# ViT block on one core: second-layer chunks, weight pieces and late attention steps moved within the first FFN's order

## The reference, cut to what matters

```python
h = einsum('bhid,oi,od->bho', x, weighted_sum, weight)      # x (8, 512, 256, 4) -> h (8, 512, 256)
h = h + attn(layernorm(h))                                  # 16 heads of 16, rope, unit q and k, softmax, projection
# FFN with 8 experts, hidden size 1024, every expert on every token, weighted by its gate
x_flat = layernorm(h)
probs = sigmoid(x_flat @ Wg + bg); weights = probs * (probs > 0.5)
hid = relu(einsum('td,edh->eth', x_flat, W1) + b1)
out = einsum('te,etd->td', weights, einsum('eth,ehd->etd', hid, W2) + b2)
h = h + out
```

## Time and profile before

| what | value |
|---|---|
| three runs | 1892.27, 1889.27 and 1893.55 us; median 1892.27 us |
| the profiled execution | 1891.92 us, of which the span from first to last instruction 1890.1 us |
| TensorE matmuls (PE) | 96% of the span busy |
| VectorE (DVE) | 69% |
| ScalarE (ACT) | 57% |
| GpSimd (POOL) | 6% |
| mean granted TensorE clock | 0.989 |

### The profile page before, as it was taken

How to read it: one execution, slowest core, us unless ns; L and a number is a source line. 1 busy time by engine, 2 the same in 40 slices (tenths; PEclk the granted TensorE clock), 3 DMA queues, 4 the chain that set the end, 5 groups by cost and what they waited for, 6 DMA issues and landing times.

```text
span 1890.1 us, 33337 instructions
## 1 busy us (share of the span) xinstructions
PE 1813.9 (96%) x13036; PEld 1173.0 (62%) x13036; DVE 1312.3 (69%) x2469; ACT 1076.7 (57%) x1658; POOL 111.6 (6%) x92
## 2 busy tenths in 40 slices
PE   5689899999999999999999999999999999999999
PEld 4157445775567655776557755677556775566666
DVE  7868645688865888558875788758886588863333
ACT  3745777446654566446664466544765456654444
POOL 1013323200000000000000000000000000000000
PEclk9789999999999999999999999999999999999999
DMA  4332552415122331234312242221512323223221
GB/s 166 112 112 90 147 180 99 168 51 151 69 89 101 84 140 68 69 121 113 112 68 90 79 134 90 89 98 71 156 68 70 121 70 111 89 72 117 92 104 42
DMA packets 103979, 192.40 MB, mean 102 GB/s; under 512 B 67448, under 2 KB 80656, under 8 KB 87440
## 3 DMA queue, kind: packets, MB, share of 16 engines
q1 hardware_dynamic: 103824, 190.28, 30.5%
HBM read 153.55 MB, written 20.97 MB: 92 GB/s over the span
## 4 chain that ended last, share of the span: by engine, by line
PE 81%; DVE 5%; issue 3%; ACT 3%; DMA 2%; DVEq 0%; ACTq 0%; SPq 0%
PE bank_h L1069 32%; PE bank_f L1088 11%; PE bank_f L1090 10%; PE bank_f L1091 10%; PE bank_o L975 4%; PE bank_s L950 4%; PE bank_s L855 3%; PE bank_s L856 3%; PE bank_s L857 3%; DMA qt<-probs 2%; ACT hh L832 1%; PE bank_m L987 1%; PE bank_s L1023 1%; PE bank_m L864 1%; PE bank_o L864 1%
## 5 line engine op out<-in xcount | busy, mean ns | idle before, releaser
L1069 PE MATMUL bank_h<-x,w1s 128*128 128x512 f16 x3072 | 749.7, 381 | 2.4 <-ACT hh L832 2.4
L829 ACT ACTIVATE h<-bank_h,b1s 128x512 f32<-128x512 f32 x512 | 352.2, 688 | 539.9 <-PE bank_h L1069 470.3
L1088 PE MATMUL bank_f<-w2s,hh 128*128 128x256 f16 x2048 | 560.2, 274 | 6.0 <-DVE acc L1362 5.9
L1090 PE MATMUL bank_f<-w2s,hh 128*128 128x256 f16 x2048 | 558.4, 273 | 0.0
L1091 PE MATMUL bank_f<-w2s,hl 128*128 128x256 f16 x2048 | 558.3, 273 | 0.0
L1069 PEld LDWEIGHTS bank_h<-x,w1s 128*128 128x128 f16 x3072 | 289.3, 99 | 296.2 <-issue 23.2
L1144 DVE TENSOR_TENSOR hl<-h,hh 128x512 f16<-128x512 f32 x448 | 309.9, 695 | 136.6 <-PE bank_f L1091 107.0
L832 ACT ACTIVATE hh<-bank_h,b1s 128x512 f16<-128x512 f32 x512 | 349.7, 683 | 0.0
L1088 PEld LDWEIGHTS bank_f<-w2s,hh 128*128 128x128 f16 x2048 | 201.3, 98 | 106.9 <-issue 48.0
L1090 PEld LDWEIGHTS bank_f<-w2s,hh 128*128 128x128 f16 x2048 | 200.6, 98 | 49.7 <-issue 0.3
L1091 PEld LDWEIGHTS bank_f<-w2s,hl 128*128 128x128 f16 x2048 | 200.4, 98 | 23.3
(11 more groups left out here) (215 smaller groups left out, 1800.2 us busy)
## 6 DMA issues: line engine op xcount, KB each, us to landing
w1s<-w_parts SPq DMA_DIRECT2D x56, 1024.0 KB, 4.8
w2s<-w_parts SPq DMA_DIRECT2D x56, 1024.0 KB, 4.8
raw<-in_w_dram SPq DMA_DIRECT2D x16, 1024.0 KB, 6.3
xraw<-in_x_t_dram SPq DMA_DIRECT2D x30, 512.0 KB, 6.1
w_parts<-w1s SPq DMA_DIRECT2D x8, 1024.0 KB, 8.8
w_parts<-w2s SPq DMA_DIRECT2D x8, 1024.0 KB, 10.6
out_dram<-acc SPq DMA_DIRECT2D x16, 256.0 KB, 6.0
w1s<-in_x_t_dram SPq DMA_DIRECT2D x2, 512.0 KB, 9.0
```

What stands on the lines that cost most here:

```text
L829: act.activation(h32[n % 2][:], bank_h[n % 2][:, :], ACT.Relu, bias=b1s[:, e, m:m + 1]).then_inc(h_hi.sem, 1)
L1069: last = pe.matmul(bank_h[n % 2][:, :], w[:, wp, k, m * P:(m + 1) * P], x16s[fb % 2][:, xp, k, :], start=(k == 0 and wp + xp == 0), stop=( ...
L1088: pe.matmul(o, high, w[:, 0, m, :], start=(m == 0 and t % 2 == 0), stop=False, skip_group_check=True)
L1090: pe.matmul(o, high, w[:, 1, m, :], start=False, stop=False, skip_group_check=True)
```

## The change

It changes only the list of the first FFN (the second of the four lists), and how ScalarE reorders it:

- `behind=(2 * HM, 3 * HM)`: `f2 16` stands behind `f1 20`, directly ahead of `f2 17`, and `f2 24` stands behind `f1 28`, directly ahead of `f2 25`.
- `exps_first` takes `maxima`, `share` and `scales` out of ScalarE's list, on which it does nothing, so that more steps are neighbours, and a `parts` step now also lets a following `f1` (its two relus) pass. On ScalarE this puts `f1 9` ahead of `parts 9`, `f1 12` ahead of `parts 11`, `f1 21` ahead of `parts 12`, `f1 22` ahead of `parts 14`, `f1 23` ahead of `parts 15`, `f1 30`, `f1 38` and `f1 46` ahead of `parts 18`, `22` and `26`, and the exps of `scores` 1, 3, 13, 25 and 27 ahead of the relus of `f1` 26, 27, 34, 42 and 43. The lists of batches 1 to 7, and the one that stands ahead of the first FFN, come out as before.
- `att_turn 3` stands ahead of `split_ahead 0` and `f2 50`, and with it `project 3` ahead of `parts 31` and `f2 51`.
- For expert 7, `share 7` and `scales 7` stand ahead of `f1 51` and `project 0`.

```diff
-FIRST_ATT = [0.0, 1.7, 2.5, 3.4]
+FIRST_ATT = [0.0, 1.7, 2.5, 2.85]
...
-              6: (0.6, 2.0, 3.2, 3.5, 4.3, 5.0, 5.7, 6.4)}.get(e, (0.6, 2.0, 3.7, 3.9, 4.4, 5.0, 5.7, 6.4))
+              6: (0.6, 2.0, 3.2, 3.5, 4.3, 5.0, 5.7, 6.4),
+              7: (0.6, 2.0, 2.95, 2.97, 4.4, 5.0, 5.7, 6.4)}.get(e, (0.6, 2.0, 3.7, 3.9, 4.4, 5.0, 5.7, 6.4))
...
-    def merge(waiting, done=0):
+    def merge(waiting, done=0, behind=()):
...
-            if c >= LAG:
+            if c >= LAG and c - LAG not in behind:
+                if c - LAG - 1 in behind:
+                    order.append(("f2", c - LAG - 1))
                 order.append(("f2", c - LAG))
...
-    return first, merge(attention_order(first_ffn=True) + prep, done=4), merge(attention), merge([])
+    return first, merge(attention_order(first_ffn=True) + prep, done=4, behind=(2 * HM, 3 * HM)), merge(attention), merge([])
...
-    order = list(order)
-    for passed, step in (("parts", ("scores",)), ("f1", ("scores", "gates"))):
+    order = [step for step in order if step[0] not in ("maxima", "share", "scales")]
+    for passed, step in (("parts", ("scores", "f1")), ("f1", ("scores", "gates"))):
```

## The result

The changed kernel runs in a median of 1896.3 us (1892.92 to 1897.93, 17 runs), the kernel before in 1892.46 us (1889.27 to 1894.39, 17 runs beside it). The ratio is 1.0016, with a 95% interval of 1.0009 to 1.0023: 3.0 us slower, 1.7 to 4.4 (the two medians themselves lie 3.8 us apart). That lies within the 0.2% of "no change", on the slow side of it, and 4.3 us above the upper end of the range that was given. The profiled execution took 1895.68 us, 0.6 under the median.

What follows compares the result with a forecast made beforehand. TensorE, busy 96% of the span, bounds the kernel, so only its waits can be won. Gains of 0.7 (front) and 2.5 us (attention turn) take 3.2 off 1891.92, 1888.7; median put at 1889.0 us, range 1885.7 to 1892.0.

Steps and rivals of the forecast that it cites:

- What bounds, and which waits go: First FFN: TensorE busy 96%; listed waits of 8.1 us plus 1.7 us of lower clock, 9.8 us at most to win.
- that rival: Raw loads landing late before share 4 and share 7: up to 4.8 us cost, 1893.9 us; chance 0.07.
- I take 1.9: VectorE's chain up to scales 3: 1.9 us late because pieces 9 and 11 stand behind relus; bounds 0 and 2.8.
- 2.6 us less the lateness: Front part, up to share 4 and f2 24: gain is 2.6 us less the lateness of VectorE's chain, 0.7 us left.
- The rule: VectorE and GpSimd instructions exclude each other on SBUF; moved chain meets subtractions at better places, lateness 1.2 us, sum 1888.3.
- A new wait of 0.7: Before mix_ahead 1: TensorE there at 338.85, split's first low half ends at 339.6; 2.4 to 2.5 us gain left.
- The prediction's own sign of being wrong: Wrong if scales 3 ends near 202.2, or the first FFN's end moves by less than 2 or over 4.5 us.
- 1.7 us more: At project 3: with its wait cut from 1.82 to 0.65, the clock stays at 2.4 GHz, gaining 1.7 us.
- the clock falls elsewhere: Clock falls before f1 24 or still at project 3: 1.7 us lost, partly covered, 1890.5 us; chance 0.15.
- the chain does not matter: VectorE makes up its lateness; the front gives up to 2.6 us, together 5.1: 1887.2 us; chance 0.30.
- The minor steps: share 7 sooner: a wait of 0.5 to 0.6 replaces 0.64, 0.2 us gained; f2 16 moved: 1.3 us taken alone.
- the step gives 1.3 us: f2 16 behind f1 20: f1 20 fills the wait for acc 1, worth 1.3 us taken alone.

Runs made afterwards that it cites:

- late_pass: Changed kernel, but relus pass pieces only from piece 12 on, so pieces 9 and 11 stand where they stood before; 1.0009 of the kernel before.
- low_on_dve: Changed kernel with the low halves of hidden chunks 54 to 56 made on VectorE instead of GpSimd; 0.9985 of the kernel before.
- att_only: Kernel before with only att_turn 3 and project 3 sooner; 1.0020 of the kernel before.
- share_only: Kernel before with only share 7 and scales 7 sooner; 0.9993 of the kernel before.
- behind_only: Kernel before with only f2 16 moved behind f1 20 and f2 24 behind f1 28; 0.9987 of the kernel before.
- split_first: Changed kernel with split_ahead 1 ahead of ln2 on VectorE; 0.9996 of the kernel before.

## Why the prediction was wrong

- **What bounds, and which waits go: right.** Every wait of the earlier trace rows went or shrank but the one before `f1 24`, whose growth was forecast too, and new ones stand at the steps named. `share 3` waits 1.58 us (1.4 predicted), `share 4` 1.29 (1.3), `share 7` 0.53 (0.5 to 0.6), `project 3` 0.75 (0.65) at the full clock. The raw loads landed in time: `maxima 9` began 220.09 - 213.27 = 6.8 us after low piece 15 was made, as before; that rival can be dropped.
- **"I take 1.9" for the lateness of VectorE's chain: mis-sized.** It is 3.1, or 2.8 without the later start of this execution, the upper bound that the prediction had given. The part worked out from relus and pieces was right: `late_pass`, which puts just that back, returned 1.95 us of it. What failed is the sentence that put `scales 3` behind the chain by that sum alone. Chunk 21's relus pass piece 12, its subtraction on GpSimd comes earlier with them and holds the stack's lows for 1.0 us. So `f1 24` started at 209.10 instead of 207.85, after a wait of 2.91 instead of 2, and the front's "2.6 us less the lateness" became a loss of 0.15 us at `f1 29` instead of a gain of 0.7.
- **The rule was weighed with the wrong sign.** The rows at `gw` showed the hold, and I guessed that a moved chain would meet the subtractions at *better* places (1.2 us of lateness). It met them at worse ones, at 202 us and again at 330, 334 and 339 us. The rule itself held: the low pieces went from 1.28 us to 2.18 and 2.24 beside a GpSimd subtraction, and back to 1.28 when the subtraction was taken off GpSimd. The Trainium skill (SBUF — State Buffer, "Who interferes with whom") says that a VectorE instruction with two SBUF inputs contends with a GpSimd instruction that reads SBUF. The trace agrees. Where the subtractions fall has to be worked out, and they had moved with the relus.
- **"A new wait of 0.7" before `mix_ahead 1`: the step that failed most.** It measured 2.44. I had carried `ln2` and `split_ahead 1` over with "the same pieces and adds ahead of it as before". They are the same, but pieces 30 and 31 took 1.9 us more together and the normed rows 0.9, while the one hold of before, 0.95 in `y`, was gone: 1.8 us more in all, and the wait was forecast 1.7 too short. TensorE was there at 339.2, near the 338.85 reckoned. `mix_ahead 1` went from 341.94 to 341.63, 0.6 us sooner when counted from the first mix, the missing fall included, where 2.4 to 2.5 were to be left. `low_on_dve` shows this cause, and `att_only` that the step on its own loses 3.8 us. The prediction's own sign of being wrong came out, the end of the first FFN moving by less than 2 us.
- **"1.7 us more" for the clock at `project 3`: a chance taken for a property.** The kernel before has that fall in its profile; `share_only`, with the same wait of 1.83 us, has none. The change then brought a wait of 2.44 us at `mix_ahead 1`, and with it more time at the lower clock (0.9872 against 0.9883 without that wait). The rival "the clock falls elsewhere" had the mechanism, priced at one fall in place of another, not at more falls than before.
- **The rival "the chain does not matter"** falls: VectorE made nothing up.
- **The minor steps: one held, one in part.** `share 7` sooner is worth 0.4 us in the trace of `share_only`, where 0.2 was forecast (by the time 1.3, -0.4 to 2.8). Of the two moved `f2`, "the step gives 1.3 us" for `f2 16` holds only as a shift: in `behind_only` these 1.3 us stand before `f1 23`. Its gain by the time is 2.5 us (0.8 to 4.2), where its expectation had 1.4.

## What to carry to other kernels

When steps are moved on one engine, list what its results start on the *other* engines, and look which instructions those will now run beside: a 1.2 us subtraction on GpSimd was worth 0.9 to 1.0 us of VectorE's chain at each of four places, and one edit that kept three of these off VectorE's way returned 5.9 us. Which of the two engines pays turned here on who began first, by 0.1 or 0.2 us. A wait can cost more than its length, because the clock may fall at it; but that isn't told by the length alone, for 3.1 us before `f1 23` cost no clock that the means of the runs show, and 2.44 at `mix_ahead 1` did. And a fall seen in one profile is one throw: compare runs at the same granted clock before giving it a price.

If a version is to be kept, it is the changed kernel with `split_ahead 1` ahead of `ln2` and with relus passing no pieces before piece 12, or none at all: 0.9980 and 0.9982 of the kernel before, about 0.9965 of the changed one. Not tried: filling the wait of 2.8 to 3.1 us before `f1 23` or `f1 24`, which is the largest that is left in them.

## What was not expected of the hardware

- A low piece on VectorE and a subtraction on GpSimd that began together, or GpSimd 0.12 us ahead, cost VectorE 0.90 to 0.96 us and GpSimd next to nothing: its own took 1.21 and 1.16 us, where the mean of the 64 is 1.19. With VectorE 0.22 us ahead (the kernel before at 329.73) it was the other way round: 1.28 us for VectorE, 2.07 for GpSimd.
- The same wait is followed by the 1.2 GHz level in one execution and not in the next: 1.82 us at `project 3` with a fall and 1.83 with none, 3.11 us before `f1 23` with a fall and 3.10 with none, 2.11 and 2.12 us in batches 6 and 7 with one and 2.11 in batch 6 of `split_first` with none. The runs of one kernel lie up to 5 us apart (1892.92 to 1897.93), and the longer ones read the lower clock.
